# Moving the gating of a mixture of experts into the attention ahead of it

## What is computed

```python
h = h + _L0_attn_ref(_layernorm(h))
h = h + _L0_ffn_ref(_layernorm(h), ...)      # 16 experts, relu, top 2
...
h = h + _L3_attn_ref(_layernorm(h), ...)
h = h + _L3_ffn_ref(_layernorm(h), ...)      # causal attention with rotary angles, then 8 experts, silu, top 2
```

```python
gate_logits = x @ gate_w + gate_b
topk_vals, topk_idx = jax.lax.top_k(gate_logits, 2)
topk_w = jax.nn.softmax(topk_vals, axis=-1)
h = jax.nn.relu(jnp.einsum('bsh,ehf->bsef', x, w1) + b1)
expert_out = jnp.einsum('bsef,efh->bseh', h, w2) + b2
```

## Time and profile before

| what | us |
|---|---|
| median of 3 runs | 1049.62 |
| lowest, highest run | 1047.46, 1064.9 |
| the profiled execution | 1049.9 |
| its span in the profile | 1048.0 |
| first attention, about | 120 to 222 |
| `entry` and experts of the first layer | 222 to 345 |
| last attention, about | 840 to 925 |
| `entry` and experts of the last layer | 925 to 1048 |

### The profile page before, as it was taken

One profiled execution on the slowest core, in us unless ns is written; L12 is line 12 of the kernel. 1 busy time (PEld: TensorE's weight loads), 2 busy tenths in 40 slices (PEclk: granted clock), 3 DMA queues, 4 the chain that ended last, 5 costly groups with the idle time before them and its releaser, 6 DMA issues. The chain is left out here.

```text
span 1048.0 us, 17078 instructions
## 1 busy us (share of the span) xinstructions
PE 904.0 (86%) x6611; PEld 454.4 (43%) x6611; DVE 649.8 (62%) x1734; ACT 368.5 (35%) x645; POOL 223.3 (21%) x291
## 2 busy tenths in 40 slices
PE   1988788979997865997898879999998799979998
PEld 0577566652323334762455333333333344443333
DVE  4977556567675264997467554555653555677665
ACT  0113533234543332223435314444444023443222
POOL 2600022215336031430230320121223402100000
PEclk9998899899999986998998968999999688989999
DMA  9300300000000001000000000000000000000000
GB/s 305 84 1 2 98 2 2 2 2 1 1 1 1 1 1 43 2 2 1 1 1 1 1 1 1 1 1 1 2 1 1 1 1 1 1 2 1 5 6 11
DMA packets 11477, 15.41 MB, mean 15 GB/s; under 512 B 8268, under 2 KB 9324, under 8 KB 10398
## 3 DMA queue, kind: packets, MB, share of 16 engines
q1 hardware_dynamic: 9976, 13.20, 4.2%
q10 hardware_dynamic: 1418, 1.09, 0.4%
HBM read 13.76 MB, written 0.52 MB: 14 GB/s over the span
## 5 line engine op out<-in xcount | busy, mean ns | idle before, releaser
L622 DVE TENSOR_REDUCE mx<-PS 128x2 f32<-128x1024 f32 (+3 forms) x104 | 109.6, 1095 | 103.8 <-PE PS L440 96.9
L582 ACT ACTIVATE arena<-PS 128x1024 f32<-128x1024 f32 (+3 forms) x104 | 91.0, 923 | 130.3 <-PE PS L470 130.3
L1217 DVE TENSOR_TENSOR arena<-arena,PS 128x512 f32<-128x512 f32 (+1 forms) x144 | 97.0, 684 | 45.0 <-ACT arena L1192 40.8
L1121 PE MATMUL PS<-XT,late 64*128 64x512 f32 (+1 forms) x288 | 101.9, 650 | 11.0 <-PEq L2502 6.6
L485 PE MATMUL PS<-arena 128*64 128x512 f32 (+3 forms) x416 | 99.8, 569 | 0.5 <-DVE arena L683 0.4
L465 PE MATMUL PS<-arena 32*128 32x512 f32 (+4 forms) x416 | 78.6, 622 | 9.7 <-ACT arena L559 7.4
L1192 ACT ACTIVATE arena<-PS,f_b_sb 128x512 f32<-128x512 f32 x96 | 61.8, 685 | 63.2 <-PE PS L1121 61.8
L1153 PE MATMUL PS<-arena,late 128*64 128x512 f32 (+1 forms) x288 | 81.6, 617 | 0.9 <-DVE arena L1217 0.7
L440 PE MATMUL PS<-arena 32*128 32x512 f32 (+4 forms) x416 | 72.8, 643 | 5.8 <-DVE arena L615 2.6
L1121 PEld LDWEIGHTS PS<-XT,late 64*128 64x128 f32 (+1 forms) x288 | 28.2, 183 | 62.5 <-ACT arena L1192 41.5
L1192 ACT ACTIVATE arena<-PS 114x512 f32<-114x512 f32 x48 | 27.4, 596 | 67.6 <-PE PS L1123 66.9
(11 more groups left out here) (423 smaller groups left out, 1632.9 us busy)
## 6 DMA issues: line engine op xcount, KB each, us to landing
arena<-in_rel SPq DMA_DIRECT2D x4, 1024.0 KB, 11.8
late<-in_edges SPq DMA_DIRECT2D x2, 1024.0 KB, 11.4
late<-in_w_f_w SPq DMA_DIRECT2D x3, 342.0 KB
arena<-in_adj SPq DMA_DIRECT2D x1, 1024.0 KB, 6.7
late<-in_w_f_w SPq DMA_DIRECT2D x2, 512.0 KB, 3.7
Cc<-in_consts SPq DMA_DIRECT2D x1, 916.0 KB
arena<-in_ids ACTq DMA_DIRECT2D x1, 800.0 KB
late<-in_w_f_w SPq DMA_DIRECT2D x4, 128.0 KB, 3.8
```

The source lines that it names most:

```text
L582: nc.scalar.activation(PT[:, s % 2, p, :, queries(c)], PS[:, a:a + 2, queries(c)], ACT.Exp, scale=scale).then_inc(exp_done.sem, 1)
L622: v.reduce_max(mx[:, g % 2, c, 2 * p:2 * p + 2], PS[:, a:a + 2, keys(c)], axis=AX.X).then_inc(max_done.sem, 1)
L1121: ins = nc.tensor.matmul(PS[0:rows, up_bank(n), :], w1(i)[r], XT2[r, b * S:(b + 1) * S], start=True, stop=True)
L1217: nc.vector.tensor_tensor(HG[0:rows, n % 4, :], ha, PS[0:rows, gate_bank(n), :], ALU.mult).then_inc(gated_done.sem, 1)
```

## The change

For the first and the last experts `entry` is no longer called. A new class `Gating` holds an `Entering` for the norm and the parts of the gate arithmetic. Quarters 0 to 2 are normed, turned and projected inside the attention ahead, as soon as their heads are added: in the first attention in groups 3, 5 and 7, in the last one in groups 2, 3 and behind the last group. The gates of the first half (quarters 0 and 1) are made in the attention's last groups and turned at its end. The rest moves into `experts`: quarter 3 is normed at the start (root after tile 2), turned and projected around tiles 6 to 9, and the second half's gates are made by VectorE after the tiles 10, 11 and 13 to 18, two `weigh` steps per tile, and turned at the tiles `T + 6` and `T + 8`. The products that nothing reads and the copies by VectorE (`last_gates_out`) fall away. The projection now always uses the first 64 rows of `XT2`.

In the first attention:

```diff
+        normed_at = {2 * q + 3: q for q in range(B - 1)}
...
+            if g in normed_at:
+                units += [("N", normed_at[g], 0)]
...
+            if kind == "N":
+                return projection_out, gating.read(g)
...
                     within(g)
+                    if g in normed_at:
+                        chain.turn(eng, normed_at[g], slot(("N", normed_at[g], 0)))
                     if g + 2 < G:
                         proj(g + 2)
                     across(g)
+                    if g in normed_at:
+                        gating.project(eng, normed_at[g], bank(("N", normed_at[g], 0)) + 1)
                 outs(G - 1, 0)
                 outs(G - 1, 1)
+                a = slot(("G", 0, 0))
+                for q in range(2):
+                    gating.turn_gates(eng, q, a + q)
...
+                    if g in normed_at:
+                        chain.root(eng, normed_at[g], 0)
                     if g >= 1:
                         outs(g - 1)
                     draw(eng, g)
+                    if g == G - 2:
+                        gating.tops(eng, 0)
+                        gating.places(eng, 0)
+                    if g == G - 1:
+                        for i in range(12):
+                            gating.weigh(eng, 0, i)
                     if g + 2 < G:
                         elu(g + 2)
+                    if g + 1 in normed_at:
+                        eng.wait_ge(heads_added.sem, at(heads_added, 4 * g - 1))
+                        chain.sums(eng, normed_at[g + 1], 0)
+                    if g in normed_at:
+                        gating.logits(eng, normed_at[g], bank(("N", normed_at[g], 0)) + 1)
```

In the last attention (TensorE, ScalarE, VectorE; GpSimd does `centre` at c = 1 and `apply` at c = 3):

```diff
+            if c == 0 and g >= 2 and gating is not None:
+                units += [("R", g - 2, 0)]
...
                         cols(s)
+                        if gating is not None and steps[s][1] == 1 and steps[s][0] >= 2:
+                            gating.project(eng, steps[s][0] - 2, bank(("R", steps[s][0] - 2, 0)) + 1)
...
+                    if c == 0 and g >= 2 and gating is not None:
+                        after.turn(eng, g - 2, slot(("R", g - 2, 0)))
...
+                if gating is not None:
+                    after.turn(eng, G - 2, slot(("R", G - 2, 0)))
+                    a = slot(("G", 0, 0))
+                    for q in range(2):
+                        gating.turn_gates(eng, q, a + q)
+                    gating.project(eng, G - 2, bank(("R", G - 2, 0)) + 1)
...
+                    if gating is not None and c == 0 and g >= 2:
+                        after.turned_out(eng, g - 2, bank(("R", g - 2, 0)))
+                    if gating is not None and c == 2 and g == G - 1:
+                        gating.exps(eng, 0)
...
+                    if gating is not None and g >= 2 and c == 1:
+                        gating.logits(eng, g - 2, bank(("R", g - 2, 0)) + 1)
...
+                    if gating is not None and g == G - 1 and c == 2:
+                        gating.tops(eng, 0)
+                        gating.places(eng, 0)
...
+                    if gating is not None and g == G - 1 and c == 3:
+                        for i in range(12):
+                            gating.weigh(eng, 0, i)
                 outs(G - 1)
+                if gating is not None:
+                    gating.logits(eng, G - 2, bank(("R", G - 2, 0)) + 1)
```

In `experts`:

```diff
+        TURN, PLACE, WEIGH = 6, 10, 13
+        GATES = T + LAG + 2
...
+                    if gating is not None:
+                        if s == TURN:
+                            gating.chain.turn(eng, B - 1, 7)
+                        if s == TURN + 2:
+                            gating.project(eng, B - 1, 7)
+                        if s == GATES:
+                            eng.wait_ge(out_added.sem, a0 + 1)
+                            gating.turn_gates(eng, 2, 6)
+                        if s == GATES + 2:
+                            eng.wait_ge(gates_sent.sem, gating.gates_in(2))
+                            gating.turn_gates(eng, 3, 6)
...
+                        if n == TURN + 1:
+                            gating.chain.turned_out(eng, B - 1, 7)
+                        if n == WEIGH:
+                            gating.exps(eng, 1)
+                        if n == GATES + 1:
+                            gating.gates_out(eng, 2, 6)
+                        if n == GATES + 3:
+                            gating.gates_out(eng, 3, 6)
...
+                if gating is not None:
+                    gating.chain.sums(eng, B - 1, 0)
...
-                        if n == 1:
+                        if gating is None and n == 1:
                             entered["last_gates_out"]()
+                        if gating is not None:
+                            if n == 2:
+                                gating.chain.root(eng, B - 1, 0)
+                            if n == TURN + 3:
+                                gating.logits(eng, B - 1, 7)
+                            if n == PLACE:
+                                gating.tops(eng, 1)
+                            if n == PLACE + 1:
+                                gating.places(eng, 1)
+                            if WEIGH <= n < WEIGH + 6:
+                                gating.weigh(eng, 1, 2 * (n - WEIGH))
+                                gating.weigh(eng, 1, 2 * (n - WEIGH) + 1)
```

More of the change, by code:

```diff
@@ L393, in softmax_attention @@
         entered.received()
-        if after is not None:
+        for signal in (turned_copied, tiles_turned):
+            signal.count += B
+        if gating is not None:
+            gating.opened()
+            after = gating.chain
+        elif after is not None:
             after.opened()
@@ L949, in _ @@
                         nc.scalar.copy(CT[:, p, :], PS[:, 6 + p, :]).then_inc(ctx_ready.sem, 1)
+                for q in range(2):
+                    gating.gates_out(eng, q, bank(("G", 0, 0)) + q)
             @block.vector
@@ L1068, in _program, with experts @@
     out_added = Signal(ctx, nc, "out_added")
-    def experts(E, T, rows, w1, w2, act_fn, gate, base, dst, b1=None, w3=None, b2=None, store=False, aside=None, block=None, entered=None, between=None, after=None):
+    def experts(E, T, rows, w1, w2, act_fn, gate, base, dst, b1=None, w3=None, b2=None, store=False, aside=None, block=None, entered=None, between=None, after=None, gating=None, late=False):
         tiles = [(b, i) for b in range(B) for i in range(T)]
@@ L1084, in experts, with _ @@
         LAG = 4
+        TURN, PLACE, WEIGH = 6, 10, 13
+        GATES = T + LAG + 2
         with nullcontext(block) as block:
+            if late:
+                @block.sync
+                def _(eng):
+                    eng.wait_ge(late_in.sem, 16 * len(LATE))
+            if gating is not None:
+                @block.gpsimd
+                def _(eng):
+                    gating.chain.centre(eng, B - 1, 0)
+                    gating.chain.apply(eng, B - 1, 0)
             if aside is not None:
@@ L1115, in up @@
                     b, i = tiles[n]
+                    if gating is not None and i == 0 and b == B - 1:
+                        eng.wait_ge(turned_copied.sem, gating.chain.copied(b))
                     if n >= RU:
@@ L1225, in _ @@
                         eng.wait_ge(turned_done.sem, t0 + b + 1)
+                        if gating is not None and b == B - 1:
+                            gating.chain.complete(eng, b)
                         nc.vector.tensor_tensor(dst[:, y, :], PS[:, out_bank(b), 0:TB * D].rearrange("p (t d) -> p t d", d=D), base[:, y, :], ALU.add).then_inc(out_added.sem, 1)
@@ L2088, in project, with l0_ffn @@
             return [(slice(0, P), w("a0_wqk")[j * D:(j + 1) * D, n * P:(n + 1) * P], XT2[j * D:(j + 1) * D, b * S:(b + 1) * S])]
-        linear_attention(2 * B, lambda g, j: g // 2, project, MV[:], lambda g, p: 2 * (g % 2) + p, X, H, 1e-9)
-    def l0_ffn(after):
-        then = {}
+        linear_attention(2 * B, lambda g, j: g // 2, project, MV[:], lambda g, p: 2 * (g % 2) + p, X, H, 1e-9, gating)
+    def l0_ffn(gating, after):
         with nc.Block() as block:
-            entry([Norm(H, X)], turned=XT2[:], proj=[(w("f0_gate"), 16, L16, row("f0_gate_b"))], gates=(16, None), late=True, block=block, then=then)
             experts(16, 16, P, lambda e: w("f0_w1")[:, e // 2 * P:(e // 2 + 1) * P], lambda e: w("f0_w2")[:, e * D:(e + 1) * D],
-                    ACT.Relu, one_gate, X, Y, b1=lambda e: w("f0_b1")[:, e:e + 1], b2=b2h[:, 0], aside=bins_folded, between=keys_drawn, block=block, entered=then, after=after)
+                    ACT.Relu, one_gate, X, Y, b1=lambda e: w("f0_b1")[:, e:e + 1], b2=b2h[:, 0], aside=bins_folded, between=keys_drawn, block=block, gating=gating, late=True, after=after)
     def l1_attn(entered):
```

195 lines of the change are left out of this document (172 added, 23 removed).

## The result

The changed kernel took 1065.64 us (median of 4 executions, 1063.87 to 1079.2) beside 1050.15 for the kernel before (4 executions, 1047.46 to 1064.9): a ratio of 1.0145, 95% interval 1.0088 to 1.0203. Forecast were 1046 and the range 1033 to 1059. It is slower, by more than its measurement is uncertain and by less than 2%. (All ratios leave disturbed executions out; the medians and means are over all of them.)

The account below looks back on a forecast made before the run. TensorE, busy 86%, was read as the bound, with serial gate chains of 22.5 and 21.1 us between attentions and experts. 1049.9 - 31.8 + 9.0 + 5.0 + 7.8 + 6.0 = 1045.9, say 1046 us; range 1033 to 1059.

Parts of the forecast that it names:

- The entries: Serial stretches between attention and experts, first and last layer: removed apart from a new ramp, gaining 16.2 and 15.6 us.
- First attention: Norm, turns and projections added in groups 3, 5 and 7: +9.0 us, bounds 4.2 to 12.
- (c): First attention, groups 3 and 5: the next diagonals wait for logits, which stand behind elu on VectorE; +1.8 us each.
- The rule on the clock: TensorE waiting between batches is throttled again and starts each next batch slow; the trace agreed in one group of seven.
- the likeliest case: The summed forecast for the whole kernel: 1046 us, by itself 1040 to 1052, chance 0.5.
- a rival with three falls of 3.1 us: TensorE falls to 1.2 GHz after new logits waits in both attentions: 9.3 us plus 1 for ramps, 1056; chance 0.2.
- Untouched stages: Stages between first experts and last attention, whose code is the same: predicted change 0.
- First experts: Quarter 3's norm and the second half's gates added among the expert tiles: +5.0 us, bounds 2.1 to 9.
- Last experts: The same gate work, plus ScalarE table loads, added in the last layer's experts: +6.0 us, bounds 2.1 to 9.
- the two table loads: Last experts, ScalarE: switching between exponential and Silu brings two loads of 1.28 us, costing the stage +1.6 with 0.5 besides.
- Last attention: Turns, projections and gate work added in groups 2, 3 and the tail: +7.8 us, bounds 5 to 10.
- tail +4.6 (4.0): End of last attention: gates' exponential delays step 15, then root and weigh precede the last outs; +4.0 us.

Follow-up runs that it names:

- fill: Changed kernel plus unread products in the first attention: four ahead of outs of groups 3, 5, 6, 7, eight after each logits projection; 1062.4 us, ratio 1.0065.
- l3_only: Kernel before with only the last layer's part of the change, the first layer restored: median 1057.5 us, ratio 0.9997.
- before_again: The kernel before, unchanged, run and profiled a second time: median 1054.9 us, ratio 0.9979.
- tail: Changed kernel with ScalarE's exponential of the gates moved behind step 15's exponential in the last attention: median 1064.5 us, ratio 1.0063.
- fill_end: fill plus twelve unread products behind the first attention's last gate turns, ahead of the experts; against the kernel before: median 1055.5 us, ratio 0.9974.
- fill_end_again: The same kernel as fill_end, repeated on another chip against the kernel before: median 1058.5 us, ratio 1.0028.
- early: Changed kernel with the first attention's logits moved ahead of elu(g + 2) on VectorE: median 1066.5 us, ratio 1.0168.

## Why the prediction was wrong

**The entries** (-16.2 and -15.6): right, -16.4 and -15.2, ramps included.

**First attention** (+9.0): the step was right and is not what was measured. At full clock (fill) groups 3 to 6 take 52.8 us against 45.7 untouched (three of 11.68 and one of 10.62), +7.1 where 7.6 was summed: 4.2 and not 3.4 in groups 3 and 5 (0.6 of it the fillers themselves), 0.7 less each in groups 4 and 6. Group 7 added 1.9 in the changed kernel (1.4). Of the +17.7, then, 9.0 is the sum and 8.7 is the clock, net of the 3.1 that the first profile's own spell cost before; without the fillers' 1.2 it is 7.8 and 9.9. The (c) of that step, 1.8 a group for the wait for `logits`: moving the logits ahead gave back 0.8.

**The rule on the clock.** Weighed was the Trainium skill, "TensorE: Matmul & The Clock Gate", section HAM oscillation, by which a TensorE that waits between batches is throttled again. The profile of the changed kernel agrees with it in three groups of five (3, 4 and 6), and fill shows that four and eight products in the gaps stop it.

**The step that failed** stands under the sum's silence: the clock's cost was put at zero in "the likeliest case". It was named as a rival with three falls of 3.1 us; what argued against it, that six groups with a gap of 1.4 us had not fallen, did not carry over to the changed groups, which wait more. Which waits bring a fall stays open: 0.84 and 1.11 us one after another came ahead of the fall at 162 us, and the same two in group 5 (195.00 and 196.66) brought none; the fall at 210 came after a further 1.17. The rival's place and mechanism were right and its size was short: it counted 9.3 + 1 us in the two layers that change, and there it was 8.7 + 4.4 (the three falls in groups 3 to 6 cost 11.8 against fill; the 8.7 is net of the 3.1 that before had paid). The untouched stages were in no case at all.

**Untouched stages** (0): +9.4 in this pair of profiles, from the clock alone. A delay of 3 to 6 us brings the same, l3_only shows it without any change ahead, and before_again shows that the kernel before mostly escapes it. Part of the miss is the baseline: its first three executions had a median of 1049.62, 103 more have 1055.3. By the means over all executions the change costs 11.1 us, not 15.5.

**First experts** (+5.0): +3.2. **Last experts** (+6.0): +8.0, of which 3.6 is the work and 4.4 the clock; the two table loads took 1.28 us each as priced, what they cost the stage was not measured. So the work of both experts was summed too high, by 4.2 us in all, and the clock covered that in the last layer. **Last attention** (+7.8): +8.6, right in its sum: group 2 +2.1 (2.3), group 3 +1.9 (1.45), tail +4.6 (4.0). What ends the tail is VectorE's list, as summed: from the end of the mask (940.09) to the end of `weigh` (944.66) it takes 4.6 us, not 3.5. The place of ScalarE's exponential alone had no part in that, as tail shows. The spell in TensorE's last `outs` was not foreseen; VectorE was still at `weigh` then, so it need not have cost anything.

**By the clock's account.** Over the 103 executions of the kernel before, a time is longer by 8.9 us for each 0.01 of mean clock that it lacks (scatter about that line 1.9 us). At its own mean clock of 0.900 the kernel before would by that line take 1072.5; the changed one took 1067.4, 5.1 us less (standard error 0.9), and the stage table without its clock terms (16.0 - 8.7 - 9.4 - 4.4) gives -6.5. The sum had said -4.0. It is a correlation, extrapolated a little below the slowest executions of before (0.904), and the delayed kernels do not obey it well: they lie 6.4 to 11.8 us above the line with delays of 3.0 to 5.7. It supports, and doesn't prove, that the work alone would have been a small gain. Against it: fill_end and fill_end_again, with the same work and their clock held up, lie only 1.1 and 0.4 us under the line, and the price of their fillers in the first attention, about 1.2 us in groups 3 and 5 and at most 2.4 in group 7, does not quite make up the difference.

**What stays open**: what fixes the pattern of spells in the middle stages. Their start matters (the delays), but starts 5.1 us apart had the same pattern (before, before_again), and no rule for the good starts came out of 18 profiles. Fillers in the first attention of the kernel before were not tried.

## What to carry to other kernels

Work moved beside a dense TensorE stage is paid for twice, in its own time and in the gaps that it opens, after which the engine ran at half its clock for some 10 us here, three times: list the gaps that each new wait adds to those already there, and put products that nothing reads into them before judging the change (here that was worth all of the 1.4%, within the noise, though the fillers cost some 3 us themselves). Take many executions of the kernel before, since one profile at a clock of 0.925 hid a mean 6 us higher. Stages far behind the change may take another time too: in 15 of 18 profiles here one of them took 5 or 10 us more than in the first. Before moving work ahead of a wait, see whether some other engine's list is full up to the end of the stage: in the last attention's tail it was, and two changes of order gained nothing.

## What was not expected of the hardware

Identical instructions from 476 to 602 us took about 0, 5 or 10 us more in 18 profiles, and nothing between. Four executions with a delay of 3.0 us had a mean 13.3 us higher. Two to eight products in gaps of about 1 us kept the clock up in the first attention in all eight profiles; twenty in an idle stretch of 6.6 us ahead of the second experts did so in one of two. The same two waits, 0.84 and 1.11 us, came ahead of a fall in one group and of none in another. And 0.76 us taken off a wait in each of two groups (early) was worth nothing until the clock was steady, and then about 0.8 a group.
